# Stores of the first pass on SyncE's queue, loads on GpSimd's, and loads of Y that wait for transposes

## Chip, cores, metric

One core of one Trainium2 chip. The metric is the device time of one execution in microseconds, the median of the runs.

## What is computed

From x (4096 x 512), keys and values (4096 x 512), an adjacency matrix (4096 x 4096, zeros and ones) and weights (512 x 512), in fp32:

```python
q, k, v = x @ Wq.T + bq, key @ Wk.T + bk, value @ Wv.T + bv
scores = (q @ k.T) / 4096 ** 0.5 * adj
scores = where(abs(scores) < 1e-5, -1e9, scores)
a = softmax(scores) @ v @ Wm.T + bm
x1 = layernorm(x + a)
out = layernorm(x1 + relu((adj @ x1) @ W.T + b))
```

## The kernel before

fp32 operands are split into a high and a low fp16 part; a product is three passes of matmuls (high by high, low by high, high by low). Wq and Wk are multiplied first, so that the scores are T times keys, T = x Wq^T Wk and a bias.

**Stages.** A preparation (to about 125 us) makes T for all rows and stores it in `t_dram`. The first pass (`first_period(q)`, q = 0 to 15) takes two tiles of 128 rows a period, against the first half of the keys (2048 columns, two groups `gr`). The second pass (`second_period(q)`, q = 16 to 31, i = q - 16) takes the same rows against the other half, merges the two halves of the softmax, and makes x1 and Y = x1 W1^T behind them. A last stage multiplies the adjacency matrix by Y.

**A period on TensorE** (`period`): the scores of 256 rows by 1024 columns a group as seven block products P1, P7, P6, P2, P5, P4, P3 of six matmuls each (`scores`, L1028), from sums of quarters of T (`left`) and of keys (`KG`), in two groups. Between them stand the four parts of `weigh(g, part)` (L1049), 12 matmuls each: probabilities of tile g, transposed (`PT`), by the values `V`. With g0 = 2(q - 1) and g1 = g0 + 1: `weigh(g0, 0)` follows P3 of group 0, `weigh(g1, 0)` P3 of group 1; g1's other three parts stand in group 0 of the next period. In the second pass come `project` (L1060, reads `UT`) and `rows_product` (L1073, reads `x1T`), two of each a period.

**Around it.** ScalarE copies products between banks (`seed`), takes magnitudes, exponentials and the high half of the probabilities (`prob_high`), which waits for the transposed high half of the tile before (`ph_in`). VectorE adds, masks with `adjh`, finds the row maxima, and makes the low half (`prob_low`, waits `pl_in`). `Phl` has one buffer, `PT` two. Each engine takes its instructions in the order written. ScalarE's `t_high` makes the next `left` in the second group and waits until the last one is stored (`left_st`). 

**Queues.** SyncE (SP) issues the transposes, all of them in DMA: `turn_high` and `turn_low` (L434, L439) of the probabilities, `turn_merged_*` (UT), `turn_x1_*` (x1T) and `adj_part` / `adj_tile` (AT, from `adj_bf`), and loads of x, of left factors and of stored outputs. It stands still where it waits, with all that follows. GpSimd (POOL) issues the rest. Its order in a first-pass period:

```python
load_adj(q, 0); store_left(q); load_t(q + 1); load_adj(q, 1)
store_x_bias(2 * (q + 1)); store_adj(q, 0); store_adj(q, 1)
load_chunk(...)            # 2 <= q < 6; another one below, 1 <= q < 5
store_first(2 * q - 3); store_x_bias(2 * (q + 1) + 1)
store_second_keys(q - 7); store_second_values(q - 7); load_second(q - 6)
store_first(2 * q - 2)
```

`store_x_bias` stores x with its bias row for the second pass, `store_adj` the 16-bit adjacency tile into `adj_bf`, `store_first` the first half's output into `o_dram`, `store_left` the split left factors; `load_second`, `store_second_keys` and `store_second_values` split the second half of keys and values in eight steps from q = 7 on, `load_chunk` reads them once more for their maxima, and `load_right` reads the keys back into `KG` at the end of the pass. `load_second_values` reads the second half of V (four chunks of 1 MB), `load_y` reads Y back (seven chunks of 1 MB), `load_adj` an adjacency half-tile; it waits until the one before is stored and masked.

## Time and profile before

| | |
|---|---|
| median of 3 runs | 2213.93 us (2209.04 to 2215.26) |
| profiled execution | 2206.61 us, span 2204.8 us |
| TensorE busy, granted clock | 90% of the span, 0.954 |
| VectorE, ScalarE, GpSimd busy | 70%, 40%, 13% |
| DMA queue q1 (SyncE's) | 179.36 MB, 39.8% of 16 engines' span |
| DMA queue q0 (GpSimd's) | 212.36 MB, 32.6% of 16 engines' span |

Times are from one execution, in us from the span's start. L is a line of the kernel before. An engine's idle time stands with what released it; "issue" is a wait for which the profile names nothing. The granted clock is a share of 2.4 GHz; at 1.2 GHz it reads 0.50. The busy share of DMA is a mean over 16 engines. SPq in the chain is SyncE issuing. "x12" counts instructions.

### The profile page before, as it was taken

To read this page: it belongs to the slowest core of one execution; us is meant where nothing else is said; L and a number is where in the kernel's file an instruction comes from. 1 tells how busy PE (TensorE), PEld (TensorE's weight loads), DVE (VectorE), ACT (ScalarE), POOL (GpSimd) and SP (SyncE) were. 2 spreads that over 40 slices of the span, in tenths; PEclk is the share of its full clock that TensorE was granted. 3 is DMA by queue.
4 is the path that set the end of the run, shared out by engine and by line. 5 is a ranking of instruction groups with operands and counts; after the bars stand their busy time and mean duration, and the time that the engine had idled before them with its cause. 6 is when DMAs were issued, how large, how long until landed. Compare 5 with 4: busy or idle time off the path is not lost.

```text
span 2204.8 us, 26352 instructions
## 1 busy us (share of the span) xinstructions
PE 1976.7 (90%) x8859; PEld 886.1 (40%) x8859; DVE 1543.3 (70%) x3203; ACT 873.7 (40%) x1166; POOL 283.2 (13%) x451
## 2 busy tenths in 40 slices
PE   8967777789998888969999999999999489999998
PEld 5423333334443333424444444443444134444443
DVE  7986566667777675537777777776777234888887
ACT  6764343345555454435554454544555110000000
POOL 5011111112221122100010001000011000000000
PEclk9998899899999999989999999999999699999999
DMA  8546777777878878677877788768787958455452
GB/s 304 206 134 171 168 189 187 162 189 208 223 195 223 219 192 244 170 174 164 179 179 184 173 180 170 183 160 160 162 175 179 231 105 274 119 139 141 119 128 72
DMA packets 556006, 393.21 MB, mean 178 GB/s; under 512 B 479728, under 2 KB 483824, under 8 KB 554096
## 3 DMA queue, kind: packets, MB, share of 16 engines
q1 hardware_dynamic: 501008, 179.36, 39.8%
q0 software_dynamic: 54880, 212.36, 32.6%
q8 instruction: 63, 1.03, 0.2%
q14 instruction: 55, 0.45, 0.1%
HBM read 190.32 MB, written 117.44 MB: 140 GB/s over the span
## 4 chain that ended last, share of the span: by engine, by line
PE 55%; DMA 15%; DVE 13%; issue 8%; ACT 5%; SPq 4%; DVEq 0%; ACTq 0%
PE ps L1049 17%; PE ps L1188 15%; PE ps L1028 14%; DMA PT<-Phl 11%; PE ps L1060 3%; PE ps L1073 3%; DMA UT<-Uhl 2%; ACT prob L1397 2%; SPq L435 2%; DVE prob L1944 2%; ACT Phl L1405 2%; PE ps L1143 1%; DVE left L1795 1%; DVE prob L1956 1%; DVE small L1950 1%
## 5 line engine op out<-in xcount | busy, mean ns | idle before, releaser
L1049 PE MATMUL ps<-V,PT 128*128 128x512 f16 x3072 | 733.9, 391 | 112.7 <-issue 112.7
L1028 PE MATMUL ps<-KG,left 128*128 128x512 f16 x2688 | 633.1, 384 | 48.6 <-ACT ps L1385 36.1
L1049 PEld LDWEIGHTS ps<-V,PT 128*128 128x128 f16 x3072 | 306.5, 100 | 501.9 <-issue 161.1
L1028 PEld LDWEIGHTS ps<-KG,left 128*128 128x128 f16 x2688 | 264.1, 99 | 380.1 <-issue 76.2
L1972 DVE SCALAR_TENSOR_TENSOR Phl<-prob,Phl 128x2048 f16<-128x2048 f32 x64 | 146.7, 2292 | 239.3 <-DMA PT<-Phl 144.2
L1392 ACT ACTIVATE small<-prob 128x512 f32<-128x512 f32 x256 | 159.6, 629 | 334.7 <-DVE prob L1944 315.0
L1385 ACT ACTIVATE ps<-ps 128x512 f32<-128x512 f32 x192 | 111.6, 581 | 190.1 <-PE ps L1028 190.0
L1405 ACT ACTIVATE Phl<-prob 128x2048 f16<-128x2048 f32 x64 | 122.0, 1907 | 138.1 <-DMA PT<-Phl 129.1
L1956 DVE CUSTOM_DVE_ANT_0 prob<-prob,small 128x512 f32<-128x512 f32 x256 | 173.7, 688 | 2.9
L1950 DVE TENSOR_SCALAR small<-small,eps_s,neg_s 128x512 f32<-128x512 f32 x256 | 138.4, 550 | 47.2 <-ACT small L1392 45.5
L1632 ACT ACTIVATE p<-ps 128x512 f32<-128x512 f32 x14 | 8.4, 598 | 348.0 <-PE ps L1188 348.0
L1397 ACT ACTIVATE prob<-prob,neg_max,inv 128x2048 f32<-128x2048 f32 x64 | 133.7, 2089 | 21.1 <-DVE neg_max L1965 21.1
L1060 PE MATMUL ps<-Wvm,UT 128*128 128x512 f16 x384 | 93.6, 396 | 28.1 <-DMA UT<-Uhl 26.2
L1944 DVE SCALAR_TENSOR_TENSOR prob<-ps,c_scaled,adjh 128x512 f32<-128x512 f32 x128 | 95.8, 748 | 25.9 <-PE ps L1028 24.3
L1073 PE MATMUL ps<-W1T,x1T 128*128 128x512 f16 x384 | 92.6, 393 | 17.5 <-DMA x1T<-x1hl 17.5
L2149 DVE SCALAR_TENSOR_TENSOR z_out<-ps,inv_vw,x_in 128x512 f32<-128x512 f32 x32 | 24.0, 751 | 111.2 <-PE ps L1060 111.2
L1188 PE MATMUL ps<-Y,AT 128*128 128x512 f16 x448 | 99.0, 379 | 0.0
L1944 DVE SCALAR_TENSOR_TENSOR prob<-prob,c_scaled,adjh 128x512 f32<-128x512 f32 x128 | 94.3, 748 | 4.5
L981 PE MATMUL ps<-xT,Aq 128*128 128x512 f16 x384 | 84.8, 379 | 1.5 <-DVE xT L1757 1.5
L1188 PE MATMUL ps<-Ta,S 128*128 128x512 f16 x336 | 79.4, 379 | 2.6 <-DVE S L2384 1.9
L1188 PE MATMUL ps<-Tb,S 128*128 128x512 f16 x336 | 79.4, 379 | 0.0
L729 POOL DMA_DIRECT2D o_dram<-z_out x32 | 18.2, 568 | 414.5 <-ACT z_out L1410 414.5
(238 smaller groups left out, 2159.1 us busy)
## 6 DMA issues: line engine op xcount, KB each, us to landing
adjh<-in_adj POOLq DMA_DIRECT2D x64, 512.0 KB, 8.8
adj_bf<-adjh POOLq DMA_DIRECT2D x64, 512.0 KB, 7.5
left_dram<-left POOLq DMA_DIRECT2D x16, 896.0 KB, 8.4
xraw<-in_x_t SPq DMA_DIRECT2D x8, 1024.0 KB, 9.2
t_dram<-tq POOLq DMA_DIRECT2D x8, 1024.0 KB, 5.5
x_in<-in_x SPq DMA_DIRECT2D x32, 256.0 KB, 4.3
t<-t_dram POOLq DMA_DIRECT2D x32, 256.0 KB, 8.4
xb_dram<-x_in POOLq DMA_DIRECT2D x32, 256.0 KB, 5.4
```

The source lines that it names most:

```text
L1028: last = nc.tensor.matmul(ps[:, bank, :], left[:, s, k, d * P:(d + 1) * P], KG[gr][:, RIGHT[k], m, d, :], start=(first and n == 0), stop=( ...
L1049: last = nc.tensor.matmul(ps[:, BU + b, :], PT[:, b, s, m, :], V[:, v, m, :], start=(m == 0 and n == 0), stop=(m == MT - 1 and n == 2))
L1060: last = nc.tensor.matmul(ps[:, BX, :], UT[:, n % 2, s, k, :], Wvm[:, m, k, :], start=(q == 0), stop=(q == 3 * KD - 1))
L1073: last = nc.tensor.matmul(ps[:, BX, :], x1T[:, s, k, :], W1T[:, m, k, :], start=(q == 0), stop=(q == 3 * KD - 1))
L1188: last = nc.tensor.matmul(ps[:, bank, :].rearrange("p (s d) -> p s d", s=2), left(m), right(m), start=(m == 0), stop=(m == NP - 1))
L1392: nc.scalar.activation(small[:, o % 2, :], prob[:, b, c * C:(c + 1) * C], ACT.Abs).then_inc(s_abs, 1)
L1397: nc.scalar.activation(prob[:, b, :], prob[:, b, :], ACT.Exp, bias=neg_max[:, n, half:half + 1], scale=inv[:, half:half + 1], accum_out=ro ...
L1405: nc.scalar.activation(Phl[:, HI, :], prob[:, b, :], ACT.Copy, scale=P_SCALE).then_inc(p_hi, 1)
L1944: nc.vector.scalar_tensor_tensor(out=into, in0=src, scalar=c_scaled[:, half, n:n + 1], in1=adjh[:, b, c * C:(c + 1) * C], op0=ALU.add, op1 ...
L1950: nc.vector.tensor_scalar(small[:, o % 2, :], small[:, o % 2, :], eps_s[:, half:half + 1], neg_s[:, half:half + 1], ALU.is_lt, ALU.mult).t ...
L1956: nc.vector.tensor_tensor_reduce(out=prob[:, b, c * C:(c + 1) * C], in0=prob[:, b, c * C:(c + 1) * C], in1=small[:, o % 2, :], scale=1.0, ...
L1972: nc.vector.scalar_tensor_tensor(out=Phl[:, LO, :], in0=prob[:, b, :], scalar=P_SCALE, in1=Phl[:, HI, :], op0=ALU.mult, op1=ALU.subtract). ...
```

## The change

All stores of the first pass, the loads of T and the first loads of x go to SyncE's order; adjacency, chunk, key and value loads stay on GpSimd's. The stores of the second pass stay on GpSimd (with other semaphores). SyncE also takes `w1_raw` and the second half of V. On ScalarE `first_scaled(2i - 2)` for i = 1 comes later, on VectorE `c_first(4)`. The loads of Y get waits for transposes (`ul_in`: merged tiles, `pl_in`: probabilities). The other lines replace semaphores (`t_st`, `key_in`, `s_w`, `s_wm` are used again) and are left out.

```diff
+                sp.wait_ge(xt_lo, NG)
+                sp.wait_ge(t_st[0], 16)
+                load_t(0)
+                for n in range(2):
                     load_x_first(n)
+                def first_start():
+                    store_left(0)
+                    for b in range(2):
+                        sp.wait_ge(t_st[b], 16 * (NG // 2))
+                    load_t(1)
+                    for n in range(2):
+                        store_x_bias(n)
+                    for n in range(2, 4):
+                        load_x_first(n)
+                    for b in range(2):
+                        store_adj(0, b)
+
+                def first_period(q):
+                    if q + 1 < NP:
+                        load_t(q + 1)
                     if q == 1:
+                        for n in range(2, 4):
+                            store_x_bias(n)
                         for n in range(4, 6):
                             load_x_first(n)
                     turn_high(2 * q - 2)
                     turn_low(2 * q - 2)
-                    if q + 2 < NP:
+                    if 2 <= q and q + 1 < NP:
+                        store_x_bias(2 * (q + 1))
+                    if FIRST_STEP <= q < FIRST_STEP + STEPS:
+                        store_second_keys(q - FIRST_STEP)
+                    store_left(q)
+                    for b in range(2):
+                        store_adj(q, b)
+                    if 2 <= q and q + 2 < NP:
                         load_x_first(2 * (q + 2))
                     turn_high(2 * q - 1)
                     turn_low(2 * q - 1)
+                    if q >= 2:
+                        store_first(2 * q - 3)
+                    if q + 1 < NP:
+                        if q == 1:
+                            store_x_bias(4)
+                            load_x_first(6)
+                        store_x_bias(2 * (q + 1) + 1)
                     if q + 2 < NP:
                         load_x_first(2 * (q + 2) + 1)
+                    if FIRST_STEP <= q < FIRST_STEP + STEPS:
+                        store_second_values(q - FIRST_STEP)
+                    if q == NP - 1:
+                        sp.wait_ge(left_st, 16 * NP)
+                        load_left(NP, False)
+                    store_first(2 * q - 2)
+                    if q == NP - 1:
+                        load_left(NP, True)
...
+                def load_second_values(c):
+                    if c < MC - 1:
+                        sp.wait_ge(p_use, (MC - 1) * (NT - 1) + c + 1)
+                    else:
+                        sp.wait_ge(o_mm, NT)
+                    sp.dma_start(V[:, :, c * TC:(c + 1) * TC, :], vp_dram[:, :, c * TC:(c + 1) * TC, :])\
+                        .then_inc(s_w[c], 16)
...
+                    if i == 1:
+                        load_second_values(1)
                     turn_high(2 * q - 2)
                     turn_low(2 * q - 2)
+                    if i == 1:
+                        load_second_values(2)
+                        load_second_values(3)
...
                     turn_low(2 * q - 1)
+                    if i < 2:
+                        store_first(2 * q - 3)
+                    if i == 0:
+                        sp.wait_ge(kp_st, 16 * STEPS)
+                        sp.wait_ge(v1_st, 16 * STEPS)
+                        sp.dma_start(w1_raw[:, :, :], w1_t.rearrange("(k p) o -> p k o", p=P)).then_inc(s_wm, 16)
...
+                    if i == 0:
+                        sp.wait_ge(v1_st, 16 * STEPS)
+                        load_second_values(0)
...
                 pool.wait_ge(x_sq, NG)
                 for b in range(2):
                     load_adj(0, b)
                 store_t(7)
+                for q in range(1, NP):
                     for b in range(2):
+                        load_adj(q, b)
                     if 2 <= q < 6:
                         load_chunk(2 * (q - 2) + 1)
                     if 1 <= q < 5:
                         load_chunk(2 * (q - 1))
                     if q == FIRST_STEP - 1:
                         pool.wait_ge(kv_mx, 4 * MC)
                     if FIRST_STEP - 1 <= q < FIRST_STEP + STEPS - 1:
                         load_second(q + 1 - FIRST_STEP)
+
+                pool.wait_ge(kp_st, 16 * STEPS)
+                for k in range(NB):
+                    load_right(0, k)
+                for k in (P1, P7, P6, P2, P5, P4):
+                    load_right(1, k)
+                load_adj(NP, 0)
+                load_right(1, P3)
+                load_adj(NP, 1)
...
+                def second_period(q):
+                    i = q - NP
+                    if i >= 1:
+                        for b in range(2):
+                            load_adj(q, b)
+                    if i >= 3:
+                        store_y(2 * i - 5)
+                    for b in range(2):
+                        store_adj_again(q, b)
+                    if i >= 2:
+                        store_x1(2 * i - 4)
+                    if i >= 3:
+                        store_sums(i - 3)
+                    if i == NP - 1:
+                        pool.wait_ge(ul_in, 16 * (NT - TC))
+                        for c in range(3):
+                            load_y(c)
+                    if i >= 2:
+                        store_y(2 * i - 4)
+                        store_x1(2 * i - 3)
...
+                pool.wait_ge(ul_in, 16 * (NT - TC + 1))
+                load_y(3)
+                store_y(NT - 5)
+                store_x1(NT - 4)
+                store_sums(NP - 3)
+                pool.wait_ge(pl_in, 32 * NT)
+                for c in range(4, 7):
                     load_y(c)
...
                     magnitude(q, 0, C12)
-                    if i >= 1:
+                    if i >= 2:
                         first_scaled(2 * i - 2)
                     magnitude(q, 1, C11)
                     seed(q, 1, BCU)
                     seed(q, 1, BU2)
+                    if i == 1:
+                        first_scaled(2 * i - 2)
...
-                    if q + 1 < NP:
+                    if 2 <= q and q + 1 < NP:
                         c_first(2 * (q + 1))
...
                     prob_low(q - 1, 1)
+                    if q == 1:
+                        c_first(2 * (q + 1))
```

## Rows read from the trace of the kernel before

**Rows 1.** The page, part 1: busy us, share of span, instructions.

```profile
PE 1976.7 (90%) x8859; PEld 886.1 (40%) x8859; DVE 1543.3 (70%) x3203; ACT 873.7 (40%) x1166; POOL 283.2 (13%) x451
```

**Rows 2.** Windows: us, busy PE, PEld, DVE, ACT, POOL, PEclk, DMA share, GB/s.

```profile
600.00:650.00 50.00, 45.29 (x198) 19.87 (x197) 36.89 (x67) 25.01 (x32) 10.26 (x17) 0.93 0.81 214
1200.00:1250.00 50.00, 49.90 (x232) 22.39 (x231) 38.58 (x88) 25.95 (x38) 4.88 (x9) 1.00 0.79 179
```

**Rows 3.** Chain of waits, whole span: start, duration, what; first pass.

```profile
190.12 5.14 PE ps L1049 x12
...
612.90 12.56 DMA PT<-Phl
...
640.37 2.59 PE ps L1028 x12
...
659.39 13.40 DMA PT<-Phl
...
862.33 5.25 PE ps L1049 x12
```

**Rows 4.** Timeline of PE, first pass: start, us, instruction [idle before <-releaser].

```profile
297.73 4.25 PE L1049 MATMUL ps<-V,PT 128*128 128x512 f16 x12 [11.39 <-issue]
...
623.50 1.46 PE L1028 MATMUL ps<-KG,left 128*128 128x512 f16 x6
629.67 5.28 PE L1049 MATMUL ps<-V,PT 128*128 128x512 f16 x12 [4.71 <-issue]
```

**Rows 5.** Timeline of ACT, the same period.

```profile
625.48 1.91 ACT L1405 ACTIVATE Phl<-prob 128x2048 f16<-128x2048 f32 x1 [5.09 <-DMA PT<-Phl]
```

**Rows 6.** Timeline of DVE, the same period.

```profile
629.68 2.29 DVE L1972 SCALAR_TENSOR_TENSOR Phl<-prob,Phl 128x2048 f16<-128x2048 f32 x1 [6.10 <-DMA PT<-Phl]
...
643.09 0.75 DVE L1944 SCALAR_TENSOR_TENSOR prob<-ps,c_scaled,adjh 128x512 f32<-128x512 f32 x1 [1.47 <-PE ps L1028]
```

**Rows 7.** Instructions of tile PT, whole span: time from issue to landing.

```profile
DMA to landing us min/median/max: 4.2/6.2/20.1
```

**Rows 8.** Timeline of POOL, first pass.

```profile
611.76 0.56 POOL L686 DMA_DIRECT2D adjh<-in_adj  x1
...
654.37 0.58 POOL L729 DMA_DIRECT2D o_dram<-z_out  x1 [7.07 <-ACT z_out L1410]
```

**Rows 9.** The page, part 6: DMA issues, KB each, median us to landing.

```profile
left_dram<-left POOLq DMA_DIRECT2D x16, 896.0 KB, 8.4
```

**Rows 10.** Chain of waits, second pass.

```profile
1048.85 3.73 SPq L435
...
1607.27 4.60 SPq L435
```

**Rows 11.** The page, part 3: DMA queue, packets, MB, share of 16 engines.

```profile
q1 hardware_dynamic: 501008, 179.36, 39.8%
q0 software_dynamic: 54880, 212.36, 32.6%
```

**Rows 12.** Timeline of PE, start of the second pass.

```profile
959.49 2.72 PE L1028 MATMUL ps<-KG,left 128*128 128x512 f16 x6 [12.30 <-ACT ps L1385]
...
981.03 5.28 PE L1028 MATMUL ps<-KG,left 128*128 128x512 f16 x12 [5.43 <-ACT ps L1385]
```

**Rows 13.** Timeline of POOL, start of the second pass.

```profile
933.71 0.71 POOL L702 DMA_DIRECT2D V<-vp_dram  x1
```

**Rows 14.** Timeline of PE, end of the second pass.

```profile
1718.35 5.28 PE L1060 MATMUL ps<-Wvm,UT 128*128 128x512 f16 x12 [11.19 <-DMA UT<-Uhl]
...
1742.49 5.30 PE L1073 MATMUL ps<-W1T,x1T 128*128 128x512 f16 x12 [10.77 <-DMA x1T<-x1hl]
...
1758.41 4.36 PE L1060 MATMUL ps<-Wvm,UT 128*128 128x512 f16 x12 [7.83 <-DMA UT<-Uhl]
```

**Rows 15.** Timeline of POOL, end of the second pass.

```profile
1700.12 2.26 POOL L867 DMA_DIRECT2D Y<-y_dram  x3
```

**Rows 16.** Chain of waits, end of the second pass.

```profile
1702.51 15.75 DMA UT<-Uhl
```

More of the change, by code:

```diff
@@ L298, in attention_then_aggregation @@
         adj_in = [sem("adj_in%d" % b) for b in range(2)]
-        ab_st = [sem("adj_stored%d" % b) for b in range(2)]
+        ab_st = [sem("adj_first_half_stored%d" % b) for b in range(2)]
         t_ld, t_sum, t_hi, t_lo = sem("t_loaded"), sem("t_sums_made"), sem("t_hi"), sem("t_lo")
@@ L410, in _, with load_t, store_left @@
                     rows_in(G)
+                def load_t(i):
+                    wait(sp, t_lo, 2 * i)
+                    sp.dma_start(t7[:, A11:A12 + 1:A12 - A11, :], t_dram[2 * i + 1, :, :].rearrange("p (a n) -> p a n", a=2))\
+                      .then_inc(t_ld, 16)
+                    sp.dma_start(t7[:, S3:A22 + 1:A22 - S3, :], t_dram[2 * i, :, :].rearrange("p (a n) -> p a n", a=2))\
+                      .then_inc(t_ld, 16)
+                def store_left(i):
+                    sp.wait_ge(t_lo, 2 * i + 2)
+                    sp.dma_start(left_dram[i, :, :, :, :], left[:, :, :, :]).then_inc(left_st, 16)
                 def load_left(q, late):
@@ L518, in second_period @@
                         load_left(q + 1, False)
+                    if i == 0:
+                        store_first(2 * q - 2)
                     if i >= 1:
@@ L769, in store_sums @@
                     pool.dma_start(ts_dram[:, m, :, :, :], Tehl[:, :, :, :]).then_inc(ts_st, 16)
-                pool.wait_ge(xt_lo, NG)
-                pool.wait_ge(t_st[0], 16)
-                load_t(0)
-                store_t(6)
-                pool.wait_ge(x_sq, NG)
-                for b in range(2):
-                    load_adj(0, b)
-                store_t(7)
-                def first_start():
-                    for b in range(2):
-                        pool.wait_ge(t_st[b], 16 * (NG // 2))
-                    store_left(0)
-                    load_t(1)
-                    for n in range(2):
-                        store_x_bias(n)
-                    for b in range(2):
-                        store_adj(0, b)
@@ L861, in _ @@
-                for q in range(NP, 2 * NP):
-                    second_period(q)
                 def load_y(c):
@@ L1045, in weigh @@
                     if g == NT:
-                        pe.wait_ge(v_in[part], 32)
+                        pe.wait_ge(s_w[part], 48)
                     for m in range(part * TC, (part + 1) * TC):
```

184 lines of the change are left out of this document (59 added, 125 removed).

## Prediction

> **What bounds the kernel now.** I read the page first: TensorE (PE) is busy 90% of the span [rows 1]. So only idle PE time, and time at a low clock, can be won. The 50 us windows say where these are [rows 2]: in a window of the first pass (scores and probabilities against the first half of the keys, 190 to 900 us) PE is busy 45.3 us with a granted clock of 0.93, in one of the second pass 49.9 us at 1.00. DVE has 36.9 us of work there and the DMA engines 0.81 of it, so neither is full.
>
> Then the chain of waits [rows 3]. It gives the price of a block of 12 matmuls at full clock, 2.59 us. A first-pass period is 14 score products of 6 and 8 output parts of 12, 180 matmuls: 15 blocks, 38.9 us. From the first restart of PE behind a transpose (190.12) to the fourteenth next (862.33) are 672.2 us, 48.0 a period. Nine are lost in each.
>
> The PE timeline shows how [rows 4]: the last score product of the first group ends at 624.96, and `weigh(g0, 0)` starts at 629.67, 4.7 us idle, then needs 5.28 us for what takes 2.59, since the clock has fallen. In the earliest periods the idle time is 11.4 us. `weigh` needs both transposes of PT. The high one is issued at T = 612.90 and lands 12.56 us later [rows 3]. ACT waits for it (5.09 us) before it makes the next high part [rows 5], and DVE waits 6.10 us for the low one, which releases it at 629.68, T+16.8 [rows 6]. A transpose has landed in 4.2 us elsewhere; the median is 6.2 and the worst 20.1 [rows 7]. So the first pass runs in a ring: PE restarts, makes the scores, DVE and ACT make the probabilities, and 29.7 us after the restart (629.67 to 659.39) the next high transpose is issued; 17 us for the two close it.
>
> What stretches the transposes: POOL issues its backlog just ahead of them, because it stood at `store_first` until 654.37, 5 us before T' = 659.39. In the period before, the second adjacency load started at 611.76, 1.1 us ahead of T; the left factors and T's loads went out just before it, the two adjacency stores as soon as their loads land [rows 8]. A left-factor store takes 8.4 us from issue to landing [rows 9].
>
> **The change, part by part.**
>
> *Part 1, first pass.* Each period moves to SP: two `load_t`, two x stores, `store_left`, two `store_adj`, two `store_first` and in eight periods one key and one value store. Nothing is removed; POOL keeps adjacency, chunk and key/value loads. Two things follow. The adjacency loads no longer stand behind `store_first`: they start as soon as the scores are masked, ahead of 654.37, and are mostly in by T. The stores and left factors (in MB of the issues: 0.25 x, 0.9 keys, 0.9 left, 1.0 adjacency, 0.25 x load) stand behind the first pair of transposes on SP's queue, not beside it. Before that pair stand only `store_first` and `load_t`, 0.75 MB, issued about 5 us ahead. At the 214 GB/s of the window [rows 2] these take 3.5 us and are in by T. Then high lands at about T+5, low, which DVE has at T+2.3, at about T+9 (two landings at the shortest 4.2 us). PE gets there at T+12.1 (624.96 - 612.90). The wait is gone with 3 us to spare, and PE sets the period.
>
> What is late next? (a) The second pair. SP takes its instructions in order, so `turn_high(2q - 1)` is behind the 3.3 MB and behind the waits of `store_adj` (adjacency in), of the key store (DVE) and of `load_x_first` (x store landed). ACT's high part is ready at about T+9.5, and the 3.3 MB, at 264 GB/s (an estimate: 214 at a share of 0.81 [rows 2]), keep the queue 12.5 us, until T+21.5; the pair lands at about T+27. PE wants it after seven blocks and the last product, at T+31.5: 4 us to spare. (b) `left` must be stored before ACT makes the next one in the second group, about T+22: it lands near T+15. (c) DVE: between PE's P2 of the second group (DVE waits for it 1.47 us at 643.09 [rows 6]) and the issue of the next transpose are 16.3 us, which stay. PE is at P2 10.4 us after it reaches `weigh(g0, 0)`, T+22.5, so T' = T+38.8: just PE's own 38.9. DVE is the closest second.
> The second pass shows what a period costs when PE is meant to bound it: from 1048.85 to 1607.27 are eleven periods of 50.8 us [rows 10] for 228 matmuls, 49.2 us: 1.6 lost. With the same loss: 40.4 us, 7.6 less than 48.0, times 14: **106 us**. The bound from below is 38.9 (128 us), from above the present 48.0 or worse.
>
> A rule of the Trainium skill speaks against this part: DMA: Bandwidth & Descriptors, section Issuing engines are not separate DMA queues, says that DMAs of all issuing engines run on the same 16 DMA engines and interleave, and that issuing elsewhere saves only sequencer time. The same page (section Queues, rings and completion order) says that an engine goes round-robin between the queues, a packet at a time. The page of the profile has packets of 358 bytes on q1 and of 3870 on q0 [rows 11]; By the second rule the transposes' small packets lose time against a full q0 and not behind their own queue, so the two together would give the 106 us; the first alone is rival C.
>
> *Part 2, start of the second pass.* V's second half (4 x 1 MB, the first issued by POOL at 933.71 [rows 13], just ahead of a pair of transposes) goes to SP one chunk ahead of a pair, one at the end of the period before and two behind; and ACT's `first_scaled` for i = 1 comes behind seeds of the second group. PE stood 12.30 us at 959.49 behind ACT (which waited for the transposed high part) and 5.43 us at 981.03 behind a seed queued after `first_scaled` [rows 12]. With clock recovery some 21 us are there. Against it stand key loads of the last period, which POOL now issues as soon as PE frees each block, so into the transposes. I take half, **10 us** (bounds 0 and 20). The start of the first pass I cost at nothing, +-5: SP's `load_x_first` waited there for the same stores.
>
> *Part 3, end.* The first three of Y's seven loads (1 MB each) were issued at 1700.12 [rows 15]; the UT transpose issued at 1702.51 took 15.75 us [rows 16], and PE stood 11.19, 10.77 and 7.83 us [rows 14]. Now three go once the merged transposes of n = 27 have landed, before UT of n = 28 is issued, one after n = 28, three after the last PT. The wait is queued on POOL ahead of `store_y` and `store_x1`; their readers are not late. PE first reads Y behind its last `weigh`, after all of these stops, so the loads are still hidden. Of 30 us idle and 7 of slow clock much is also a dependency chain (projection, nine root steps, cast, transpose), and the A transposes stay. I take **15 us** (bounds 0 and 30).
>
> Sum: 106 + 10 + 15 = 131 us, from the profiled run's own 2206.6 to 2075. That run was 7.3 below the median of 2213.9, so I forecast **2082**.
>
> **Rivals.**
> *B, half the wait stays.* The DMA share makes 38 us of work a period (0.81 x 47), and the period is to be 40. If it is truly work and not waiting, low lands near T+15 and PE waits 3 us and loses 2.7 to the clock after each wait. Then 44 us a period, 56 us won, with 20 of parts 2 and 3: 2214 - 76 = **2137**. For it: the DMA share. Against: an engine's packets take longer when both queues are full, so there is waiting in the share, and the six periods without key steps move less.
> *C, only the order of issue changes.* The transposes are as slow as before, because the same engines carry the same bytes; only parts 2 and 3 act: **2189**. Against it: half of all PT transposes land in 6.2 us or less [rows 7], those outside the backlog. This is what the page's first rule gives.
> *D, slower: SP's queue is the new bottleneck.* `turn_high(2q - 1)` stands behind 3.3 MB and three waits. It costs nothing until its low twin lands at T+31.5, and exceeds the present 48 us when it lands after T+40.6. At 110 GB/s instead of 264 it lands at T+9+30+5 = T+44 and more with the waits, say T+45: 52.4 a period, 14 x 4.4 = 62 us lost, less 25 of parts 2 and 3: **2250**. For it: at the 8.4 us of one left store [rows 9], four such one after the other are 33 us. Against: these landings overlapped with other transfers, and a queue doesn't wait for one to land before the next starts.
>
> **How the numbers follow.** Forecast 0.58 (own range 2062 to 2105), B 0.24, C 0.06, D 0.07; 0.05 that more is won (below 2062) or that something else comes in. The range of 2060 to 2150 holds forecast and B. A measurement of this kernel can tell about 0.3% from no change: faster by more than that 0.90, within it 0.03, slower 0.07.
>
> **What would show it.** Forecast: in the first pass PE's idle before `weigh(g0, 0)` below 1 us and granted clock 1.00 in the windows from 550 us on; restarts of PE 40 to 41 us apart; high transposes of the first pair landing in under 6 us; the wait of ACT for PT gone; q1 near 250 MB and q0 near 140. The last transposes of a period take longer to issue, without cost. B: the idle is 2 to 4 us at the same place. C: median landing of the first pair still 12 us. D: the idle is before `weigh(g1, 0)`, and SP's queue waits for x or adjacency stores. Part 2: no 12 us wait before P3 in the second pass's second period; part 3: UT after 1600 us below 6 us. I'd be most wrong if DVE, 3 us from the bound by my own count, or the DMA engines (share near 0.95) set the period at 43 or more.

## The result and the profile after

The changed kernel takes 2056.5 us (median of four) where the kernel before, on the same chip and in turns with it, takes 2211.5: a ratio of 0.929 [0.924, 0.933], 155 us less. Three of the four executions took 2048.2 to 2060.7 us; the fourth took 2898.6 at a granted clock of 0.664, and such a slow one (beside and backlog3 have one each too) counts in the medians of this document but in no ratio. The profiled execution took 2052.3 us, with a span of 2050.5 (before: 2206.6 and 2204.8). The prediction was 2082 with a range of 2060 to 2150; the time lies 3.5 us below its lower end.

Both traces, cut at the same points of the program, in us (w(g,0) is the start of `weigh(g, 0)`; "project" and "rows 27" are the starts of the `project` and `rows_product` blocks, 27 being the n of the W1 product):

| stretch | before | after | difference | forecast |
|---|---|---|---|---|
| start to w(0,0) | 190.1 | 184.8 | -5.4 | 0, +-5 |
| w(0,0) to w(28,0): first pass, 14 periods | 672.2 | 546.9 | -125.3 | -106 |
| w(28,0) to the first project: passage to the second pass | 141.9 | 134.1 | -7.8 | -10 |
| first project to rows 27: second pass | 697.6 | 691.8 | -5.8 | none |
| rows 27 to rows 31: its end | 110.9 | 99.8 | -11.1 | -15 |
| after it | 392.1 | 393.1 | +1.0 | 0 |

The sum is 154.4 us less. Page, parts 1 and 3, to be read against [rows 1, 11]:

```profile
PE 1942.2 (95%) x8859; PEld 879.5 (43%) x8859; DVE 1543.1 (75%) x3203; ACT 872.1 (43%) x1166; POOL 179.2 (9%) x286
...
q1 hardware_dynamic: 544096, 252.77, 52.7%
q0 software_dynamic: 35856, 138.95, 24.1%
```

73 MB went from q0 (GpSimd's queue) to q1 (SP's), as announced. The windows that answer to [rows 2], one in the first pass and one in the second (us, busy time and count of PE, PEld, DVE, ACT, POOL, granted clock, DMA share, GB/s):

```profile
600.00:650.00 50.00, 50.00 (x233) 22.68 (x232) 42.55 (x78) 33.15 (x42) 2.35 (x4) 1.00 1.07 248
1200.00:1250.00 50.00, 49.87 (x232) 22.42 (x230) 38.91 (x89) 26.14 (x38) 4.87 (x9) 1.00 0.78 177
```

PE no longer stops in the first pass (it has no stop over 0.2 us from w(0,0) to w(28,0)) and keeps the full clock in these windows. The DMA share is over 1, and in that window PE and ACT wait for no transfer, DVE 0.6 us for one. One period of SP's queue, in place of POOL's in [rows 8] (start, us, instruction); T is the moment when its first high transpose is issued:

```profile
564.34 3.93 SPq L458 DMA_TRANSPOSE PT<-Phl  x1
568.31 1.83 SPq L462 DMA_TRANSPOSE PT<-Phl  x1
...
572.80 1.57 SPq L423 DMA_DIRECT2D left_dram<-left  x1
574.41 2.51 SPq L452 DMA_DIRECT2D adj_bf<-adjh  x2
...
578.29 5.95 SPq L458 DMA_TRANSPOSE PT<-Phl  x1
584.28 2.00 SPq L462 DMA_TRANSPOSE PT<-Phl  x1
...
603.19 4.09 SPq L458 DMA_TRANSPOSE PT<-Phl  x1
```

From T = 564.34 to T' = 603.19 are 38.85 us, PE's own 15 blocks. The stores stand between the two pairs (a pair is the high and the low transpose of one tile). ACT's and DVE's next parts, which waited 5.1 and 6.1 us for the pair in [rows 5, 6], and the landing times of all PT transposes, against [rows 7]:

```profile
571.98 1.91 ACT L1431 ACTIVATE Phl<-prob 128x2048 f16<-128x2048 f32 x1
...
573.92 2.29 DVE L2000 SCALAR_TENSOR_TENSOR Phl<-prob,Phl 128x2048 f16<-128x2048 f32 x1 [0.57 <-ACT Phl L1431]
```
```profile
DMA to landing us min/median/max: 4.3/5.5/23.8
```

ACT goes on at T+7.6 without a wait, DVE waits for ACT alone. Over the thirteen first pairs before w(2,0) to w(26,0) the high transpose lands in 5.4 us (median, 4.5 to 7.6; before: 12.6), and the pair has landed at T+7.8 (before: T+17.7). The worst transpose is not better than before. It belongs to the passage to the second pass, where the 12.3 and 5.4 us stops of [rows 12] are gone and a new one stands. PE, then SP's second pair and POOL's key loads of that period:

```profile
764.64 4.03 PE L1075 MATMUL ps<-V,PT 128*128 128x512 f16 x12 [13.36 <-issue]
...
730.54 10.20 SPq L458 DMA_TRANSPOSE PT<-Phl  x1
740.79 8.62 SPq L462 DMA_TRANSPOSE PT<-Phl  x1
...
746.39 0.72 POOL L800 DMA_DIRECT2D KG<-kp_dram  x1 [3.17 <-PE ps L1054]
747.69 0.71 POOL L800 DMA_DIRECT2D KG<-kp_dram  x1 [0.58 <-PE ps L1054]
```

POOL issues fourteen key loads of 0.5 MB from 716.95 to 751.58, each as PE frees a block, and `weigh(29, 0)` waits for the pair that was issued among them. At the end the three stops of [rows 14] (29.8 us) became one long one and two of 3.0 and 1.5 us; a further one of 5.3 us before the W1 product of n = 30 stands in both kernels. PE, the three loads of Y just ahead of it on POOL, and the chain:

```profile
1603.10 4.63 PE L1086 MATMUL ps<-Wvm,UT 128*128 128x512 f16 x12 [17.02 <-issue]
...
1589.41 2.26 POOL L869 DMA_DIRECT2D Y<-y_dram  x3 [9.54 <-DMA PT<-Phl]
```
```profile
1589.66 9.39 DMA UT<-Uhl
1599.05 4.05 issue
```

The low UT transpose of n = 28, which took the 15.75 us of [rows 16], now lands in 2.8. The one of n = 29, whose two halves took 3.1 and 2.5 us before, takes 9.4 and 12.1: the gate on the last low transpose of PT let three loads of Y go 0.25 us before it was issued.

### The profile page after: what moved, and what is told of

Its sections match the earlier page's. It is cut to its first block, busy times and chain, and to the rows that moved or that the text cites. A ratio compares the mean times of both kernels' runs of the same rounds, so it can differ in the third digit from the quotient of the medians.

```text
span 2050.5 us, 26388 instructions
## 1 busy us (share of the span) xinstructions
PE 1942.2 (95%) x8859; PEld 879.5 (43%) x8859; DVE 1543.1 (75%) x3203; ACT 872.1 (43%) x1166; POOL 179.2 (9%) x286
## 4 chain that ended last, share of the span: by engine, by line
PE 73%; DVE 9%; DMA 7%; SPq 4%; issue 4%; ACT 3%; DVEq 0%; ACTq 0%
PE ps L1075 25%; PE ps L1054 23%; PE ps L1214 16%; DMA PT<-Phl 4%; PE ps L1086 3%; PE ps L1099 3%; SPq L458 2%; DMA UT<-Uhl 1%; PE ps L1169 1%; DVE prob L1972 1%; PE ps L1007 1%; ACT prob L1423 1%; ACT Phl L1431 1%; DVE Phl L2000 1%; DVE prob L1984 1%
## 5 line engine op out<-in xcount | busy, mean ns | idle before, releaser
L1075 PE MATMUL ps<-V,PT 128*128 128x512 f16 x3072 | 710.4, 381 | 24.7 <-issue 24.7
L1075 PEld LDWEIGHTS ps<-V,PT 128*128 128x128 f16 x3072 | 301.7, 98 | 393.1 <-issue 35.3
L2180 DVE SCALAR_TENSOR_TENSOR z_out<-ps,inv_vw,x_in 128x512 f32<-128x512 f32 x32 | 24.0, 751 | 98.7 <-PE ps L1086 98.7
L1086 PEld LDWEIGHTS ps<-Wvm,UT 128*128 128x128 f16 x384 | 37.7, 100 | 74.5 <-issue 32.0
```

The source lines that it names most:

```text
L1075: last = nc.tensor.matmul(ps[:, BU + b, :], PT[:, b, s, m, :], V[:, v, m, :], start=(m == 0 and n == 0), stop=(m == MT - 1 and n == 2))
L1086: last = nc.tensor.matmul(ps[:, BX, :], UT[:, n % 2, s, k, :], Wvm[:, m, k, :], start=(q == 0), stop=(q == 3 * KD - 1))
```

## The experiments

Each has its ratio to the kernel before, measured beside it, with a 95% interval. A period is the mean of the thirteen from w(0,0) to w(26,0) of its one trace; "pair" says how long after T the first pair of a period had landed (median of the thirteen before w(2,0) to w(26,0)). The passage reaches from w(26,0) to the first project (one period earlier than in the table above, since in some experiments the first stop of the passage falls into the fourteenth period):

| experiment | us | ratio | period | pair | passage |
|---|---|---|---|---|---|
| before | 2211.5 | 1 | 48.1 | 17.7 | 188.6 |
| after | 2056.5 | 0.929 [0.924, 0.933] | 39.1 | 7.8 | 172.9 |
| later | 2125.4 | 0.964 [0.958, 0.969] | 40.8 | 9.7 | 198.9 |
| later_free | 2128.6 | 0.963 [0.958, 0.967] | 40.3 | 7.5 | 211.7 |
| free | 2198.6 | 0.993 [0.990, 0.996] | 46.2 | 16.1 | 201.6 |
| beside | 2161.5 | 0.978 [0.975, 0.981] | 46.9 | 17.7 | 176.1 |
| behind | 2069.8 | 0.939 [0.934, 0.944] | 39.5 | 7.7 | 178.4 |
| pool_early | 2083.9 | 0.941 [0.937, 0.945] | 40.7 | 12.6 | 182.6 |
| ahead | 2086.0 | 0.946 [0.940, 0.951] | 41.4 | 12.1 | 180.1 |
| beside_act | 2087.0 | 0.944 [0.938, 0.950] | 41.2 | 12.7 | 180.7 |
| backlog3 | 2136.0 | 0.968 [0.964, 0.971] | 43.2 | 7.6 | 194.5 |
| beside_act3 | 2255.6 | 1.020 [1.015, 1.025] | 51.8 | 22.3 | 186.5 |
| right | 2045.9 | 0.926 [0.922, 0.931] | 39.0 | 8.1 | 174.1 |
| v_pool | 2067.8 | 0.936 [0.932, 0.940] | 39.0 | 8.0 | 167.6 |
| early_y | 2058.4 | 0.933 [0.931, 0.936] | 39.0 | 7.9 | 178.4 |
| both | 2044.8 | 0.928 [0.925, 0.931] | 39.1 | 7.9 | 166.8 |

PE gets to `weigh(g0, 0)` at about T+12.1. With the pair in by T+9.7 the periods are 39.0 to 40.8 us, at T+12.1 to 12.7 they are 40.7 to 41.4, at T+16.1 to 17.7 they are 46.2 to 48.1, and at T+22.3 51.8. The landing of this pair thus orders the periods, but for backlog3, where another pair is late.

### From the kernel before: order alone, and the freed queue alone

*later*: the kernel before, with one reordering on GpSimd's queue.

```diff
                     if q == 1:
                         for n in range(2, 4):
                             store_x_bias(n)
+                    pool.wait_ge(ph_in, 16 * (2 * q - 1))
+                    pool.wait_ge(pl_in, 16 * (2 * q - 1))
+                    store_left(q)
```

(`store_left(q)` is taken out of its place behind the first adjacency load.)

> The kernel before, with all its stores and loads on GpSimd's queue as they were; only in a first-pass period the left store, the x and adjacency stores and what follows wait until the first pair of transposes has landed (GpSimd waits for ph_in and pl_in). Theory 1, order: what counts is that the stores are not beside the first pair of transposes, on whatever queue they are. Then the idle time before weigh(g0, 0) nearly goes, a period takes 40 to 42 us instead of 48.0, and the time is 2110 to 2135. Theory 2, queue: the stores must also be on the transposes' own queue, else they slow the second pair; then a period stays above 44 and the time above 2160. Theory 3, blocking: the adjacency loads behind store_first do the harm; then nothing is won, 2195 or more.

Measured 2125.4: hit. The fourteen periods take 569.2 us, 103 less than before and 82% of the gain, without a byte moved to another queue. Windows of 300 us of the first pass, the kernel before, then later, then after:

```profile
400.00:700.00 300.00, 270.03 (x1175) 118.59 (x1176) 220.08 (x425) 148.92 (x193) 56.13 (x90) 0.94 0.77 198
```
```profile
400.00:700.00 300.00, 291.42 (x1335) 130.88 (x1333) 251.55 (x486) 174.25 (x223) 67.64 (x109) 0.99 0.96 239
```
```profile
400.00:700.00 300.00, 300.00 (x1392) 136.06 (x1391) 260.47 (x497) 185.47 (x234) 17.47 (x30) 1.00 1.01 249
```

It does not all arrive in the total, since PE stands longer in the passage than before, ahead of a weigh:

```profile
800.47 4.85 PE L1051 MATMUL ps<-V,PT 128*128 128x512 f16 x11 [24.01 <-issue]
```

The passage grew by 10 us. Whether the backlog that POOL now issues later is what meets the transposes there, no run tells.

*later_free*: later, with POOL's `store_first` of the second tile put behind the next two adjacency loads, so that these don't wait for it.

> As later, and store_first of the second tile goes behind the next two adjacency loads, so that these are not held up (the change's order of work in the first pass, but on GpSimd's queue). Theory 1: the first pass runs as in the changed kernel, 39 to 39.5 us a period, time 2080 to 2095 (the 125 us of the first pass and no other part). Theory 2: still above 44 us a period, above 2150. Theory 3: as theory 1 here.

Missed by all three theories: 2128.6, no faster than later. Nine of the thirteen periods are at 38.8 or 38.9 us, but four are longer, one of them 49.9, so their mean is 40.3 and not 39 to 39.5. The thirteen periods got 6 us shorter than in later, the passage 13 us longer. The first pass is 16 us longer than in the kernel after (563.1 for 546.9); no run says what in the move to SP's queue brings these. *free*: that unblocking alone, in the kernel before.

> The kernel before, with only this moved: store_first of the second tile goes behind the next two adjacency loads; all other stores stay ahead of and beside the first pair. Theory 1: the high transpose still lands 10 us or more after its issue, 5 to 25 us won in all, time 2185 to 2205. Theory 3: most of the 125 us is won, time below 2120.

Hit. The thirteen periods take 25 us less, the passage 13 more. Loads that start sooner are worth 2 us a period while the stores still lie beside the first pair, against 7 for the order of the stores.

### From the kernel after: one more store of 0.9 MB, in different places

`left_copy` is a place in DRAM that nobody reads. Five kernels store the left factors there too, once a period; only the moment and the queue differ. ACT must wait for the copy before it makes the next left factors, but its idle time there is the 7.6 us in thirteen periods of the kernel after in all five.

*beside*, on GpSimd's queue, at T:

```diff
                     for b in range(2):
                         load_adj(q, b)
+                    pool.wait_ge(t_lo, 2 * q + 2)
+                    pool.wait_ge(p_hi, 2 * q - 1)
+                    pool.dma_start(left_copy[q, :, :, :, :], left[:, :, :, :]).then_inc(copy_st, 16)
```

> The changed kernel with one more store of 0.9 MB a period (a copy of the left factors to a place nobody reads), on GpSimd's queue and held until ACT's high part is ready, so that it is issued with the first high transpose, beside the pair and not behind it; nothing is left out. T1, what counts is how much direct traffic lies beside the first pair, whichever queue it is on: 0.9 MB are 3.5 us of all engines, the pair lands about 3.5 us later, near T + 12.1 where PE wants it, so the loss is 0 to 2 us a period: 2056 to 2085 us. T2, any direct transfer from another queue slows the transposes by its round-robin share, most of the 17 us of the kernel before: PE stops 3 us or more each period: 2100 or more.

*behind*, the same with the last wait on `pl_in` (the pair has landed); *pool_early*, the same without that wait (4.6 us ahead of T); *ahead*, from SP directly in front of `turn_high(2 * q - 2)`; *beside_act*, from ACT directly behind `prob_high(q - 1, 0)`.

> The changed kernel with the extra store of beside, on GpSimd's queue again, but held until the first low transpose of the period has landed, so it lies beside SP's backlog and the second pair, not beside the first; nothing is left out. T1, time beside the first pair is what costs, and 0.9 MB more in a period are free: periods of 39 to 40 us, 2050 to 2070 us. T2, the amount of direct traffic in a period or a second queue is what costs: 2100 us or more; then PE stops before the second group's weigh as well.

> The changed kernel with the extra store of 0.9 MB of the experiment beside on GpSimd's queue, held only until the left factors are ready, which is about 5 us ahead of the first high transpose in place of at it; nothing is left out. beside took 45 to 46 us a period and 2162 us, its store 14 us to land. T1, what costs is that GpSimd's queue works while the pair is being transferred: 5 of the 14 us are over by then, so 40 to 43 us a period, 2070 to 2120 us. T2, any more work of that queue in a period costs, wherever it is: 45 us or more, 2150 or more. T3, only a transfer issued with the transposes costs: periods within 0.5 us of 38.9, 2050 to 2065.

> The changed kernel with the same extra store of 0.9 MB a period as in the experiment beside (a copy of the left factors, held until ACT's high part is ready), but on SP's own queue, directly in front of the first high transpose; nothing is left out. In beside it sat on GpSimd's queue and took 45.4 to 46 us a period. T1, transfers on one queue are served in order and the fault in beside is the interleaving between two queues: the pair lands 3.5 us later (0.9 MB at 264 GB/s), low at T + 12 to 13, PE wants it at T + 12.1, so 0 to 1 us is lost a period: 2050 to 2075 us. T2, direct traffic slows a transpose whichever queue it is on: periods of 45 to 46 us as in beside, 2150 to 2170 us.

> The changed kernel with the extra store of the experiment beside (0.9 MB a period, a copy of the left factors, issued as soon as ACT's high part is made, so with the first high transpose), but issued from ACT, on a queue that carries nothing else, in place of GpSimd's; nothing is left out. beside took 45 to 46 us a period and 2162 us, the same store on SP's own queue ahead of the transpose (experiment ahead) 39.4 to 43.4 us and 2086. T1, a second queue that has work while a transpose runs takes its share of every DMA engine, whichever engine issued it: 44 to 47 us a period, 2130 to 2170 us. T2, the damage in beside is peculiar to GpSimd's queue: 39 to 42 us a period, 2060 to 2095 us.

The windows of beside and of beside_act:

```profile
400.00:700.00 300.00, 268.00 (x1199) 118.84 (x1198) 220.43 (x429) 153.91 (x195) 18.76 (x33) 0.95 1.02 218
```
```profile
400.00:700.00 300.00, 290.29 (x1337) 129.81 (x1336) 249.84 (x483) 175.87 (x223) 16.32 (x28) 1.00 1.02 258
```

behind costs 0.4 us a period and pool_early 1.6, both as T1 has it. ahead was to cost 0 to 1 us a period and costs 4.2 in the first six and 0.8 in the next seven; its time is 11 us above T1's range. beside was to cost 0 to 2 and costs 7.8 of the 9.0 that the change had won: the time of its T2, but not for T2's reason (any other queue takes its share), since beside_act, on another queue as well, costs 2.1, as its own T2 says. POOL's other loads stand at the same distances from T in beside as in the kernel after, but for one period, so they are not the cause. One period of beside (SP, then POOL), the landing of all its copies, and the window over that pair, then the same of beside_act:

```profile
599.43 4.58 SPq L460 DMA_TRANSPOSE PT<-Phl  x1
604.07 10.20 SPq L464 DMA_TRANSPOSE PT<-Phl  x1
...
599.93 0.54 POOL L835 DMA_DIRECT2D left_copy<-left  x1 [6.12 <-ACT Phl L1438]
```
```profile
DMA to landing us min/median/max: 5.6/12.5/18.0
```
```profile
600.00:615.00 15.00, 11.50 (x54) 4.99 (x52) 7.89 (x12) 5.62 (x8) 0.47 (x1) 1.00 1.26 151
```
```profile
590.21 8.35 SPq L460 DMA_TRANSPOSE PT<-Phl  x1
598.61 3.85 SPq L464 DMA_TRANSPOSE PT<-Phl  x1
```
```profile
DMA to landing us min/median/max: 4.1/7.1/8.8
```
```profile
590.00:605.00 15.00, 13.41 (x63) 5.96 (x62) 9.52 (x13) 8.06 (x9) 0.00 (x0) 1.00 1.13 263
```

In these periods the DMA engines have a share of 1.26 and move 151 GB/s with the store on GpSimd's queue, 1.13 and 263 with it on ACT's. Over thirteen such windows, the 15 us from each T, the medians are 181 GB/s (87 to 276) for beside, 280 (263 to 307) for beside_act and 271 for the kernel after. pool_early is on GpSimd's queue as well and costs less than ahead: what hurts in beside is that store at that moment, not the queue at any time. Two things are left mixed. The copy goes out 0.5 us behind the high transpose in beside and together with it in beside_act, and no run separates this from the queue. And the low rate is not a mark of GpSimd's queue: the kernel before, with that queue's stores beside the pair, moves 283 GB/s in these windows, and beside_act3 (below), with nothing added there, falls to 165 to 217 in its first four.

### More bytes: rival D and its counterpart

*backlog3*: three more such stores behind `store_left` on SP's queue, 2.7 MB more ahead of the second pair.

```diff
                     sp.dma_start(left_dram[i, :, :, :, :], left[:, :, :, :]).then_inc(left_st, 16)
+                    for copy in range(3):
+                        sp.dma_start(left_copy[copy, i, :, :, :, :], left[:, :, :, :]).then_inc(left_st, 16)
```

> The changed kernel with three more stores of 0.9 MB (copies of the left factors to a place nobody reads) behind each store of the left factors on SP's queue, that is 2.7 MB more in front of each second pair of transposes; nothing is left out. T1 (rival D's mechanism): the second pair lands about 20 us after T + 14, at T + 24; PE wants it at T + 31.5, 7.5 us of slack; 2.7 MB at 264 GB/s are 10.2 us, so PE waits about 3 us a period and loses up to 2.7 more to the clock: 14 periods, 2095 to 2140 us. T2, the queue starts the transposes while the copies still run and they share the engines: the pair still lands before T + 31.5, and the time stays at 2053 to 2065. T3, the copies last beyond the next first pair too (DMA engines full): above 2140.

2136 us: the upper part of T1's range. PE stops in front of a weigh of the second group, as rival D says, and the low transpose leaves SP at 592.3, T+32:

```profile
598.04 5.28 PE L1078 MATMUL ps<-V,PT 128*128 128x512 f16 x12 [5.49 <-issue]
...
577.46 9.19 SPq L461 DMA_TRANSPOSE PT<-Phl  x1
586.70 5.62 SPq L465 DMA_TRANSPOSE PT<-Phl  x1
```

The first pair has landed at T+7.6, as in the kernel after (T+7.8). Rival D's mechanism exists, and begins somewhere below 2.7 MB beyond what the change puts there.

*beside_act3*: three stores in place of beside_act's one.

> The changed kernel with three extra stores of 0.9 MB a period from ACT's queue, 2.7 MB in all, issued as soon as ACT's high part is made, beside the first pair of transposes; nothing is left out. One such store took 39.8 to 43.6 us a period and 2087 us. T1, order in time decides whatever the queue is, and amount is what counts: 2.7 MB are 10.2 us of all DMA engines at 264 GB/s, the pair lands up to 10 us later than T + 9, PE waits 5 to 7 us and loses 2.7 more to the clock: 45 to 49 us a period, 2150 to 2210. T2, it is GpSimd's queue that hurts transposes and other queues hardly do: below 43 us a period, below 2115 us.

2255.6 us, slower than the kernel before by 2.0% [1.5, 2.5], and above T1's range: the price is 12.7 us a period, where one store costs 2.1.

```profile
605.99 4.90 PE L1078 MATMUL ps<-V,PT 128*128 128x512 f16 x12 [8.58 <-issue]
...
585.36 14.69 SPq L460 DMA_TRANSPOSE PT<-Phl  x1
```

The high transpose takes 14.7 us to leave SP, against 4 in the kernel after. The same 2.7 MB cost 4.1 us a period behind the first pair (backlog3) and 12.7 beside it, in neither case on GpSimd's queue (SP's in the one, ACT's in the other): this is the plainest form of the main result.

### The passage and the end

*right*: after, with POOL's key loads of the second group held back until the low transposes up to g = 29 have landed.

```diff
                 for k in range(NB):
                     load_right(0, k)
+                for b in range(1):
+                    pool.wait_ge(pl_in, 16 * (NT - 2))
                 for k in (P1, P7, P6, P2, P5, P4):
```

> The changed kernel, with the loads of the second group's keys (load_right(1, k), 3.6 MB) held until the transposes of tile 29 have landed. Theory: the 13.4 us that TensorE stood at 751 us before weigh(29, 0) come from the key loads beside the transposes; that stop falls below 3 us, the time falls 10 to 15 us, to 2038 to 2046. Rival: the transposes of tile 29 are late because 1.9 MB of stores stand ahead of them on their own queue; then the stop stays above 8 us and the time within 5 us of the changed kernel's 2056. Second rival: the keys now come too late for the second pass's first period and TensorE stops there as long.

The 13.4 us stop is gone, as the theory has it, and the time lies at the end of its range, but the passage is as long as in after (174.1 for 172.9), as the second rival has it: PE now stops 4.0 us for left factors, and 4.2 and 5.0 us behind ACT, which waits 12.5 us for a high transpose issued beside the postponed loads:

```profile
779.10 1.91 ACT L1433 ACTIVATE Phl<-prob 128x2048 f16<-128x2048 f32 x1 [12.47 <-DMA PT<-Phl]
```

That the gate removed the stop is likely and not shown: it is missing with the gate (right, both), and present without it in the traces of after, behind and early_y (13.4, 17.1 and 17.4 us), but v_pool, which has no gate, lacks it too.

*v_pool*: after, with the four loads of V's second half back on POOL behind the adjacency loads.

> The changed kernel with the four loads of V's second half (1 MB each) back on GpSimd's queue behind the adjacency loads of the second pass's second period, as the kernel before has them. T1, these four loads beside a pair of transposes are the 12.3 us stop of the kernel before: PE stops 8 to 12 us in that period again, and the stretch from w(28,0) to the first project grows from 134 to 142 to 147 us: 2058 to 2070 us. T2, the stop went because GpSimd's queue has no backlog of stores there any more: 2045 to 2055, the same stretch within 3 us of 134.

The ratio speaks for T1 (0.936 to 0.929, the intervals overlap by 0.001), its profiled execution against it: 2048 us, 125.4 us from w(28,0) to the first project where T1 has 142 to 147, and at the place in question 4.5 us instead of 8 to 12, where the kernel after has 4.0:

```profile
822.07 2.72 PE L1051 MATMUL ps<-KG,left 128*128 128x512 f16 x6 [4.46 <-ACT ps L1408]
```

In this trace the 12.3 us stop of the kernel before stays away although V's loads are on POOL again, so their move to SP is not what removed it; T2's reason, that GpSimd's backlog of stores is gone there, fits. The passage of v_pool is 5 us shorter than that of after, early_y, which leaves the passage alone, has it 5 us longer, and right and both, alike up to there, differ by 7. The passage depends on how the transfers happen to meet, by more than half of what part 2 was said to be worth; the other executions of v_pool (2061 to 2074 us) left no trace to be read. What part 2 brings is not settled.

*early_y*: after, with the seven loads of Y queued as before, without waiting for transposes.

> The changed kernel with its third part undone: the seven loads of Y are queued without a wait for a transpose, in the order in which the kernel before has them. T1, the third part is worth the 11 us by which the stretch from rows 27 to rows 31 got shorter: 2064 to 2070 us, with stops of 8 to 12 us before the projects of n = 28 to 30 again. T2, that stretch got shorter because the stores of the first pass's kind left GpSimd's queue or because of chance: 2052 to 2060, stretch within 3 us of 99.8.

2058.4 beside 2201.6 of the kernel before, a time in T2's range; but this chip's kernel before is 10 us faster, the ratio is 0.005 above that of after, 10 us, and the stretch from rows 27 to 31 is 108.9 us again, with the stops of before:

```profile
1588.00 4.13 PE L1082 MATMUL ps<-Wvm,UT 128*128 128x512 f16 x12 [11.54 <-DMA UT<-Uhl]
...
1610.66 4.75 PE L1095 MATMUL ps<-W1T,x1T 128*128 128x512 f16 x12 [10.77 <-DMA x1T<-x1hl]
```

T1 by the trace. The intervals of the two ratios overlap, so the time alone would not show it, but all sixteen traces do: the stretch from rows 27 to 31 is 108.9 to 112.7 us in the five kernels that load Y as before, and 98.7 to 102.0 in the eleven with the waits.

*both*: right, and `pool.wait_ge(ul_in, 16 * (NT - 2))` ahead of the last three loads of Y.

> The changed kernel with two more gates on GpSimd's queue: the right-hand keys of the second group are held back until the low transposes of the first pass's last pairs have landed (as in the experiment right), and the last three loads of Y until the UT transpose of n = 29 has landed. T1, a stop of PE in front of a transposed operand is the price of the direct loads that GpSimd queues just ahead of that transpose: the 17.0 us stop before project(29) falls to 7 us or less, the second group's last projects are not worse, and the time is 2034 to 2040 us, that is 6 to 12 below the experiment right (2046). T2, the stop only moves to the next transposes (those of n = 30 and 31) as it did in the experiment right: 2043 to 2050. T3, the loads of Y become late for their first reader behind the last weigh: above 2050, with a stop of PE before the product that reads Y.

The 17.0 us stop fell to 8.9, and the next product, where the kernel after stops 1.0 us, now waits 11.7; the 5.3 us one after it stands in both:

```profile
1584.12 4.78 PE L1089 MATMUL ps<-Wvm,UT 128*128 128x512 f16 x12 [8.85 <-DMA UT<-Uhl]
...
1608.34 4.63 PE L1102 MATMUL ps<-W1T,x1T 128*128 128x512 f16 x12 [11.67 <-DMA x1T<-x1hl]
...
1632.95 4.28 PE L1102 MATMUL ps<-W1T,x1T 128*128 128x512 f16 x12 [5.30 <-DMA x1T<-x1hl]
```

The stretch is 102.0 us, no shorter than in after: T2. Neither right nor both can be told from the kernel after by its ratio.

## Why the prediction was off, point by point

**What bounds the first pass: right.** A ring in which the first pair of transposes is late because direct transfers lie beside it. later gives 103 of the 125 us with nothing but that order, behind shows that more bytes are nearly free when they come after the pair, beside_act3 that 2.7 MB cost 12.7 us a period when they come with it. Rival C (the transposes stay slow because the same engines carry the same bytes) is refuted by later: same bytes, same queues, another order, 103 us.

**Landing of the first pair, T+5 and T+9 against a need at T+12.1: right.** Medians are T+5.4 for the high transpose and T+7.8 for the pair. In fourteen periods PE waits for neither, ACT 0.5 us and DVE 10. The sign "under 6 us" failed in the periods where the high one took up to 7.6, without cost. ahead, with 3.5 us of transfer more in front of the pair, shows about 3 us of slack in the late periods and none in the early ones, which I had read from a late period.

**The loss of 1.6 us a period: the step that failed.** The term was 14 x (48.0 - 40.4) = 106, with 40.4 made of PE's 38.9 and 1.6 that the second pass loses per period [rows 10]. Measured are 38.8 to 39.1 in thirteen of fourteen periods (41.6 in the first), and -125: 0.2 us lost a period in place of 1.6. The 1.6 was a mean over eleven periods of stops that belong to the second pass: 5.5 us before one project, for its transposed U,

```profile
1509.77 4.10 PE L1060 MATMUL ps<-Wvm,UT 128*128 128x512 f16 x12 [5.46 <-DMA UT<-Uhl]
```

and eight of 0.8 to 1.1 us (one more before a project, four before score products, three before a weigh), 12.7 of the 17 us lost in these eleven periods (kernel before). The first pass has no project and no U, and none of the other stops appeared there either: after w(0,0) PE has none over 0.2 us. I had the bound of 38.9 and "PE sets the period" in the same paragraph; a loss may be put on top only for a stop that the stretch itself has. This is 19 of the 23 us by which the sum was short (131 for 154); the start, costed at nothing, and the second pass are 11 more, parts 2 and 3 brought 6 less, the tail 1 less. The start took 183.0 to 186.8 us in the five traces whose start is the changed kernel's (after, right, v_pool, early_y, both) and 190.1 in the one trace of the kernel before, so some of its 5.4 us may be the change's own; no run separates it. The 5.8 of the second pass are within chance: PE's stops over 0.5 us in that stretch add up to 13.7 us before and 8.5 after, the longest of them, before a project, comes and goes from trace to trace, and twelve traces with this second pass have it at 686.7 to 701.7 us.

**The lower end of the range** took in the gap between 106 and 128 us (2082 - 22 = 2060) and nothing else. Together with either end of parts 2 or 3, or the start, it would have been 5 to 15 us lower.

**T' = T + 38.8: right to 0.05 us.** DVE, with 42.6 us of work in 50, did not hold PE up in the first pass.

**The second pair, 4 us to spare: there were 7.** Its high transpose was issued at T+14.0 and not held by the queue until T+21.5, and the pair had landed at T+24.3, not T+27; SP issued it at 578.29 while the left store (landed at 579.55) and the adjacency stores still moved. With that in hand, backlog3's expectation gave it 7.5 us of slack, and its time came out within the range.

**Rival B** read the DMA share as work: 0.81 x 47 = 38 us a period. After the change the share is 1.07 in the window and PE waits for nothing, and in beside it is 1.26 at 60% of the rate. So the share also counts time in which little moves, and no limit can be worked out from it. **Rival D** begins to act below 6.0 MB in front of the second pair, where the change has 3.3; its price of 110 GB/s didn't come up.

**The rule on issuing engines.** beside_act and ahead differ in the issuing engine and take 0.944 and 0.946 of the time of before, and later wins on the old queue. The Trainium skill (DMA: Bandwidth & Descriptors, section Issuing engines are not separate DMA queues) says that DMAs run on the same 16 engines and interleave whichever engine started them, and that another issuer saves only sequencer time: here the runs agree. beside and beside_act differ in the issuer and by 0.5 us in the moment, and take 0.978 and 0.944: if that is not the 0.5 us, the rule does not cover it, and the measurement decides. The round-robin between queues (same page, section Queues, rings and completion order) shows in no difference: beside_act, with its store on another queue, costs 2.1 us a period and ahead, with it in front on the same one, 2.4. What I drew from it, rival C, doesn't follow anyway: that transfers interleave says nothing about when they are let go.

**Part 2: 7.8 for 10, with luck, and not for my reason.** The two stops went and a new one of 13.4 came, in front of the pair issued among the key loads that I had named as what stands against it; whether it comes varies (v_pool), and the passage varies by 5 to 7 us from trace to trace. In v_pool's trace the 12.3 us stop is gone without V's move. **Part 3: 11.1 for 15.** early_y confirms the place and the size. UT of n = 28 lands in 2.8 us as forecast (under 6), UT of n = 29 does not: the remaining 17 us stop stands behind the gate's last step, three loads that go 0.25 us before that transpose, and moved when they were held back (both).

## What to carry to other kernels

Look for the transposes on which the ring hangs, and let direct transfers go behind them, not beside them; the queue comes second. A wait of the issuing engine on the transpose's own semaphore does it (later), but what is held back meets the next transposes if these are close, as they are where the phases change (right, both). Don't carry a loss per period from one loop to another without naming the stop in which it arises, and don't read the DMA share as a load.

## What the runs showed of the hardware that I had not expected

- A store of 0.9 MB from GpSimd's queue, let go 0.5 us behind a transpose, takes 12.5 us to land (median, 5.6 to 18.0); from ACT's queue, let go with the transpose, 7.1 (4.1 to 8.8), and from GpSimd's 4.6 us ahead of it 9.7 (8.7 to 10.8). The cost is 7.8, 2.1 and 1.6 us a period. Why is open: no run looked inside the queue or moved ACT's store by 0.5 us, and only this one shape was tried.
- The price of bytes beside a transpose is not proportional: 0.9 MB from ACT cost 2.1 us a period, 2.7 MB 12.7. Both fit the landing of the pair: T+12.7, just behind PE's need at T+12.1, and T+22.3, some 10 us behind it, and then PE's lower clock as well (0.93 granted from 400 to 700 us, for 1.00).
- The DMA share of a window can be above 1 (1.07) while PE waits for no transfer.
